# A transformer-like stack of four layers: the second mixture of experts with its inner width of 176 laid out as 256, and its table reads moved one step forward

## The reference, cut to what matters

```python
head_scores = relu(einsum('bqhd,bkd->bhqk', iq, ik))
index_scores = einsum('bhqk,bqh->bqk', head_scores, iw)
_, top_idx = top_k(index_scores, 32)              # only these keys are attended to
...
_, idx = top_k(softmax(xf @ gate_w.T) + gate_b, 2)     # two of eight experts a row
h = silu((x @ w1 + b1) * (x @ w3 + b3))           # H = 176; w1, w3: 128 x 176
oe = h @ w2 + b2                                  # w2: 176 x 128
y = sum over the two experts of weight * oe
z = the same formula with shared weights sw1, sw3, sw2, for every row
x = x + y + z
```

## Time and profile before

| | us |
|---|---|
| median of three runs | 1319.41 |
| their lowest and highest | 1312.79, 1322.32 |
| the profiled execution | 1313.25 |
| its span, first to last instruction | 1311.3 |

### The profile page before, as it was taken

One profiled execution on the slowest core, in us unless ns is written; L12 is line 12 of the kernel. 1 busy time (PEld: TensorE's weight loads), 2 busy tenths in 40 slices (PEclk: granted clock), 3 DMA queues, 4 the chain that ended last, 5 costly groups with the idle time before them and its releaser, 6 DMA issues. The chain is left out here.

```text
span 1311.3 us, 19644 instructions
## 1 busy us (share of the span) xinstructions
PE 1051.3 (80%) x4202; PEld 609.6 (46%) x4203; DVE 944.7 (72%) x2307; ACT 743.9 (57%) x1824; POOL 835.6 (64%) x602
## 2 busy tenths in 40 slices
PE   5888966399999968888888979897763249999995
PEld 4666754267777723333333333332212225555563
DVE  6999999533333437999999989999997515545574
ACT  4767755165555568776758576866422125555542
POOL 2333268657147275979898978879770677347376
PEclk9998888599999989989999999998896559999998
DMA  9991012336334233344543534353430136435345
GB/s 274 177 197 63 1 14 23 37 56 90 66 71 90 63 85 98 131 136 134 145 155 133 151 116 160 123 169 130 149 124 0 43 63 94 79 80 93 77 72 105
DMA packets 140465, 133.28 MB, mean 102 GB/s; under 512 B 14579, under 2 KB 121699, under 8 KB 140259
## 3 DMA queue, kind: packets, MB, share of 16 engines
q1 hardware_dynamic: 107106, 115.55, 31.9%
q0 software_dynamic: 33280, 16.86, 11.4%
HBM read 98.66 MB, written 31.60 MB: 99 GB/s over the span
## 5 line engine op out<-in xcount | busy, mean ns | idle before, releaser
L1854 POOL TENSOR_TENSOR ss_HC<-ss_Hs,ss_Cb 128x512 f32<-128x512 f32 x256 | 324.8, 1363 | 82.4 <-PE ss_Y L1604 61.4
L1604 PE MATMUL ss_Y<-ss_HC,g_ident 128*128 128x512 f32 x512 | 269.5, 644 | 48.9 <-POOL ss_HC L1854 41.9
L1898 DVE TENSOR_TENSOR_SCAN ss_Hs<-ss_dA,ss_dBu 128x512 f32<-128x512 f32 x256 | 297.2, 1203 | 8.0 <-ACT ss_dA L1764 8.0
L852 POOL DMA_INDIRECT rows<-m_XS,g_slot x128 | 181.1, 1415 | 69.7 <-issue 35.7
L1152 PE MATMUL m_x_UP<-g_m_w,m_x_gT 128*128 (+1 forms) x532 | 205.2, 492 | 7.2 <-issue 2.3
L1764 ACT ACTIVATE ss_dA<-ss_delta,g_A 128x510 f32<-128x510 f32 x256 | 168.1, 712 | 72.9 <-DVE ss_Hs L1898 72.7
L1604 PEld LDWEIGHTS ss_Y<-ss_HC,g_ident 128*128 128x128 f32 x512 | 91.2, 198 | 210.9 <-POOL ss_HC L1854 152.0
L1890 DVE TENSOR_TENSOR ss_dBu<-ss_duP,ss_Bb 128x512 f32<-128x512 f32 x256 | 163.7, 687 | 9.2 <-DMA ss_Bb<-bc_rows 7.5
L1172 PEld LDWEIGHTS m_x_DP<-g_m_w,m_x_hT 128*128 128x128 f32 (+1 forms) x908 | 131.3, 189 | 79.9 <-issue 37.9
L1172 PE MATMUL m_x_DP<-g_m_w,m_x_hT 128*128 (+3 forms) x908 | 161.3, 295 | 5.0 <-ACT m_x_hT L1240 2.8
L1132 POOL DMA_INDIRECT g_X<-out_rows,g_slot x64 | 100.1, 1565 | 77.9 <-DMA out_rows<-m_x_YO 55.5
(11 more groups left out here) (271 smaller groups left out, 1797.9 us busy)
## 6 DMA issues: line engine op xcount, KB each, us to landing
ss_Bb<-bc_rows SPq DMA_DIRECT2D x64, 512.0 KB, 4.9
ss_Cb<-bc_rows SPq DMA_DIRECT2D x64, 512.0 KB, 4.1
rows<-g_Z SPq DMA_DIRECT2D x2, 5031.0 KB, 49.3
m_x_G<-rows SPq DMA_DIRECT2D x156, 64.5 KB, 1.9
out_rows<-m_x_YO SPq DMA_DIRECT2D x156, 64.0 KB
g_m_w<-in_w_up SPq DMA_DIRECT2D x1, 2816.0 KB, 10.8
g_m_b<-in_b SPq DMA_DIRECT2D x1, 2160.0 KB, 11.0
g_X<-in_x SPq DMA_DIRECT2D x4, 512.0 KB, 5.8
```

The costliest lines, as they stand in the source:

```text
L852: self.nc.gpsimd.indirect_dma_start(self.XG, bass.IndirectOffsetOnAxis(self.rt.slot[k][:, t:t + 1], 0), self.XS[:, t, :], None, compute_op ...
L1604: ins = nc.tensor.matmul(Yp[:, h, :], ident[:], HC[n % 2][:, h, :], start=False, stop=n == N - 1)
L1854: nc.gpsimd.tensor_tensor(HC[n % 2][:, h, :], Hs[n % 4][:, h, :], Cb[g % 2][:, n % 2, :], ALU.mult).then_inc(hc_ready.sem, 1)
L1898: v_.tensor_tensor_scan(Hs[n % 4][:, h, :], dA[n % NA][:, h, :, :].rearrange("p s t -> p (s t)"), dBu[:, h, :], 0.0, ALU.mult, ALU.add).th ...
```

## The change

1. The second mixture is made with `padded` set. Its `chunks` become two of 128. The lower matrix's second chunk gets zeros in all its 128 rows from a GpSimd memset at the start of the attention (`last_rows`, 9 x 128 values a partition), and the load from DRAM writes 48 of them afterwards; SyncE now waits for both memsets. hid gets 80 more columns, set to zero by VectorE once for each of its two buffers at the start of the stage; TensorE waits for them (`blank`) before it begins.
2. So L1162 transposes 128 columns twice, both matmuls of L1172 contract over 128 rows, and one copy of 256 columns takes the place of L1238 and L1240.
3. On TensorE and VectorE the table is read for tile(3), at the end of `up` and of `multiply` of tile(4), so one step before its use.
4. In the attention the `sem_inc` on `passed` and `skipped` are gone.

```diff
-                                dve.sem_inc(passed, 1)
...
                     dve.wait_ge(penalty.sem, penalty.after(s))
                     dve.wait_ge(logits_ready.sem, logits_ready.after(s))
-                    dve.sem_inc(passed, 1)
...
                         pool.wait_ge(xn_ready.sem, xn_ready.after(s))
-                        pool.sem_inc(skipped, 1)
...
+        self.last_rows = each[:, :, 2 * H + (NC - 1) * D:2 * H + NC * D]
...
-    chunks = [(c, min(P, H - c)) for c in range(0, H, P)]
+    chunks = [(c, P if w.padded else min(P, H - c)) for c in range(0, H, P)]
...
-        hid = [m.sb(f"hid{v}", [P, H]) for v in range(2)]
+        hid = [m.sb(f"hid{v}", [P, NC * P if w.padded else H]) for v in range(2)]
...
                     if tile(4):
                         up(tile(4), held)
+                    if tile(3) and w.padded:
+                        place_of(nc.tensor, tile(3), held, False)
                     if tile(6):
                         down(tile(6), held)
...
+                if w.padded:
+                    pe.wait_ge(blank, len(hid))
...
-                    full = H // P * P
+                    full = sum(n for _, n in chunks if n == P)
                     ins = nc.scalar.activation(hT[v % 2][:, 0:full], HP[:, 0:full], ACT.Copy)
...
                     if tile(4):
                         multiply(tile(4), held)
+                    if tile(3) and w.padded:
+                        place_of(nc.vector, tile(3), held, False)
                     if tile(6):
                         output(tile(6), held)
...
+                if w.padded:
+                    for q in range(len(hid)):
+                        nc.vector.memset(hid[q][:, H:], 0.0).then_inc(blank, 1)
...
                 nc.gpsimd.memset(Z[:], 0.0).then_inc(cleared, 1)
+                nc.gpsimd.memset(w1.last_rows, 0.0).then_inc(cleared, 1)
...
-                sp.wait_ge(cleared, 1)
+                sp.wait_ge(cleared, 2)
```

More of the change, by code:

```diff
@@ L205, in attention @@
         x_updated = m.sig("x_updated", 2)
-        passed = m.sem("passed")
-        skipped, b_added = m.sem("skipped"), m.sig("b_added")
+        b_added = m.sig("b_added")
         def steps(eng, step):
@@ L544, with __init__ @@
 class MixtureWeights:
-    def __init__(self, g, tag, a, norm, w_router, gate_b, weights, n_shared, H, biases):
-        self.H, self.n_shared = H, n_shared
+    def __init__(self, g, tag, a, norm, w_router, gate_b, weights, n_shared, H, biases, padded):
+        self.H, self.n_shared, self.padded = H, n_shared, padded
         self.loaded = g.sig(tag + "loaded", 16)
@@ L991, in experts @@
         placed = m.sem("placed")
+        blank = m.sem("blank") if w.padded else None
         d.place(UP, HP[:, 0:P], DP[1][:, 0:P], DP[1][:, P:2 * P])
@@ L1226, in silu @@
                             act.wait_ge(h_turned.sem, h_turned.after(j - 2))
-                        ins = nc.scalar.activation(hid[v % 2][:], sg[v % 2][:, 0:H], ACT.Silu)
+                        ins = nc.scalar.activation(hid[v % 2][:, 0:H], sg[v % 2][:, 0:H], ACT.Silu)
                     ins.then_inc(silu_ready.sem, 1)
@@ L1976, in build @@
         rt = Routing(g)
-        w1 = MixtureWeights(g, "m1_", a, None, "w_router1", "gate_b1", ("w_up1", "w_down1"), T, H1, "b1")
+        w1 = MixtureWeights(g, "m1_", a, None, "w_router1", "gate_b1", ("w_up1", "w_down1"), T, H1, "b1", True)
         w_in, conv_w, conv_b = g.sb("w_in", [P, 4 * P]), g.sb("conv_w", [P, 2, 4]), g.sb("conv_b", [P, 2])
@@ L1991, in build @@
         front = outer.enter_context(ExitStack())
-        w0 = MixtureWeights(Maker(nc, front, "g_"), "m0_", a, "norm0", "w_router0", None, ("w_up0", "w_down0"), 0, H0, None)
+        w0 = MixtureWeights(Maker(nc, front, "g_"), "m0_", a, "norm0", "w_router0", None, ("w_up0", "w_down0"), 0, H0, None, False)
         consts = (ident, tri, ones, rev, masks, tile_of_half)
```

## The result

The changed kernel takes 1301.55 us (median of 4 runs, 1297.95 to 1303.74), the kernel before beside it 1317.13 (4 runs, 1312.79 to 1322.32): ratio 0.9884, 95% interval 0.9859 to 0.9909. That is 15.6 us faster. 1303.0 was forecast, with a range of 1294 to 1315. The profiled execution took 1300.29, its span is 1298.5.

The account below looks back on a forecast made before the run. TensorE's second-mixture matmuls until the last routed tile's store, then GpSimd's gathers, were taken as the bound. Routed part 14.5 us plus attention 2, less a little for clock dips, gave 16: 1319.4 to 1303, range 1294 to 1315.

Parts of the forecast that it names:

- A usual step: Second mixture, routed tile: 1.80 us in place of 2.075, saving 3.5 us in 13 steps.
- VectorE's 1.74: Second mixture: VectorE, with its sequencer as busy as before, allows 1.74 us a routed step and no less.
- The loop of 1.72: Second mixture: the chain UP, copy, DP, transposes, next UP but one takes 3.44 us for two steps, 1.72 each.
- PE's 1.7: Second mixture: TensorE's sequencer, with one table read per step as before, needs some 1.7 us a step.
- DP to UP: Second mixture, DP's weight load to the next UP's: falls from 1.11 to about 0.76 us with full 128-row passes.
- the shared tile: Second mixture, tiles without a table read: one step every 1.63 to 1.7 us, from 1.84 before.
- The first rival: Second mixture: DP's passes get no shorter, 1.91 us a step, 1311 us in all; chance 0.20.
- The read moved, not removed: Second mixture: the early read takes nothing out of TensorE's sequencer but falls under UP and the copy wait.
- The start of a pass: Second mixture's loop: a third read costs 0.8 us more, three first steps take 8.2 instead of 7.4.
- The first tiles: Second mixture's first eight tiles, 18.6 us before, four of them at half clock: 3 us saved.
- The attention: Removing the `sem_inc` before L452 saves 0.12 us of VectorE's wait in each of 16: 2 us.
- The clock: Second mixture: a rival had TensorE's clock fall to half for half the steps, 1329 us; chance 0.07.

Follow-up runs that it names:

- the reads alone: The kernel before with only the table reads on TensorE and VectorE moved one step earlier: 1316.71 us (12 runs), ratio 1.0008.
- the counts alone: The kernel before with only its six `sem_inc` of `passed` and `skipped` in the attention removed: 1314.04 us (12 runs), ratio 0.9987.

## Why the prediction was right

- *A usual step*: 1.80 was taken between 1.74 and 1.82, and 1.795 came over the same twelve steps as the 2.075; undisturbed steps take 1.754. So both halves held: VectorE's 1.74 is the bound, and more steps on it moved the time at once, and the near equals add a little at times. The loop of 1.72 and PE's 1.7 lie just under it, which the runs do not part.
- *DP to UP* 0.76, measured 0.77, and the shared tile 1.63 to 1.7, measured 1.64. The price of the passes was read from other passes of the same trace, and it held as a sum. The 0.195 for each pass is an average that hides where the time goes: the two changes between 128 and 48 rows cost 0.20 each, and two passes of 48 rows behind each other are as close as those of 128. The first rival (the passes get no shorter) is out. By the Trainium skill's "TensorE: Matmul & The Clock Gate", LDWEIGHTS (loading the stationary operand), a load takes the same time for few rows as for many. The trace agrees for the load itself: one of 48 rows takes 0.18 to 0.19 us, one of 128 rows 0.19. But that says nothing of what stands between two loads, so the rival did not follow from the page. The Trainium skill's "TensorEngine Tiling (Array Packing)", Key Properties, has the engine drain at a switch of tiling modes; a cost at the change alone, at 64 and 48 rows and not at 80, fits that. That these plain passes are such a switch is not stated there and not shown here.
- *The read moved, not removed*: right. It is hidden in full (1.11 with the reads alone is the passes' own), and the sequencer got ahead. That on VectorE it brings nothing was argued, and one run bears it out.
- *The start of a pass*: 8.2 forecast, 8.28 measured at tile 24 and 8.09 at tile 56 (8.57 at tile 40, where the clock fell). The passes are 31.2 to 32.2 against 31.7.
- *The first tiles*: 3 forecast, 3.2 in the profile. But the counts alone, with the same loop, took 16.6 there and not 18.6, so about 2 of it was the one profile's chance; the term agreed by luck.
- *The attention*: 2 was too much for what the profile shows, 0.8. The step that failed is that the time of L452's wait comes off in full: VectorE then waits longer for ScalarE at L419. With the counts alone it was 2.0, and the other profiles scatter by more than the term, so its size stays open.
- *The clock*: that it might "dip now and then" was right in size (one dip of 3.4 us after). The reason given against a fall, that TensorE never rests over about half a microsecond, left the starts out: it rests 0.99 there, and those rests are the change's own. With the reads alone, such falls took back the gain in the profiled run of 1322.03.

The sum, 16 against 15.6, is nearer than the runs can tell: their interval holds everything from 12 to 18.6. In part it is luck: by the other runs the terms for the first tiles and the attention are smaller than forecast, the profile of the change shows 12.8 in all, and the rest of the 15.6 is scatter.

## What to carry to other kernels

Where two things end at nearly the same moment, here a sequencer's string of steps and the array's passes, neither edit alone shows its worth (0.02 and 0.15 us a step, and 0.32 together): price them as a pair, and test the pair. Read the sequencers' rows as well as the engines': a table read with its register steps costs more than most arithmetic here, and at the start of a loop pass it is paid for every tile in flight; writing both loops out brought 19 us on top of the change's 16. Before padding a contraction to 128 rows, see whether another cut gives the same: 96 and 80 did. And before giving a price to each of several passes, look at the distance between every two of them: an average hid that only two changes were paid for.

## What the runs showed of the hardware

- A change between passes of 112 or 128 rows and passes of 64 or 48, in either direction, put 0.20 us more between two weight loads (0.31 in place of 0.11), at full clock. Between 80, 96 and 128 rows, and between two passes of 48 or of 64, it was 0.11.
- The load of a bounded table read mostly holds a sequencer 0.30 to 0.31 us (0.39 in the routed step of the earlier trace rows, up to 0.57 at a start of a pass), and a register step of 0.15 (TensorE) or 0.19 (VectorE) follows; a second long register step and an assert on VectorE made each step of the kernel 0.28 longer.
- In the second mixture past its first tiles, the clock fell only within 3 us of the end of a rest of TensorE of about 1 us, for 3.4 to 17.1 us, and never in the profiles without such rests. At 0.50 a step took 3.16 in place of 1.925: the pass with the fall of 17.1 us took 39.4 where the others took 33.0 to 34.6.
